# Filler matmuls ahead of the transposes in a recurrence on TensorE

## What is computed

```python
def rec_step(carry, inp):
    R, h = carry
    zt, kt, vt, bt = inp
    qh = softmax(h)
    v_old = einsum('bhij,bhj->bhi', R, kt)
    R = R + (bt * (vt - v_old))[..., :, None] * kt[..., None, :]
    h = zt + einsum('bhij,bhj->bhi', R, qh)
    return (R, h), h
```

## Time and profile before

| what | us |
|---|---|
| runs, device time | 18266.01, 18280.08, 18282.9 |
| median | 18280.08 |
| profiled execution, span first to last instruction | 18228.0 |
| median less that span | 52.1 |
| recurrence, 9936 to 14770 in the span | 4834 |
| one run, prologue included | about 604 |

### The profile page before, as it was taken

The page is one execution under the profiler, slowest core; times in us unless marked ns, Lnnn a source line. Parts: engine busy times, 40 slices in busy tenths (PEclk is TensorE's granted clock), DMA queues, the critical chain, the costliest instruction groups (busy, mean ns, idle before and its releaser), DMA issues. The chain is left out here.

```text
span 18228.0 us, 593330 instructions
## 1 busy us (share of the span) xinstructions
PE 13070.7 (72%) x262069; PEld 10252.8 (56%) x262069; DVE 10572.6 (58%) x24424; ACT 6554.5 (36%) x16019; POOL 2261.8 (12%) x1394
## 2 busy tenths in 40 slices
PE   4607778770866999999997766776677676867777
PEld 3504566660544777777775555555555565645555
DVE  6451457774125666666666777666767645446664
ACT  3101236550213666666664221111112122345541
POOL 0038200003461111111111000000000000000001
PEclk9556568875867999999998766776687697967775
DMA  0313320121332111111112112201220152177652
GB/s 20 110 26 49 72 48 21 34 76 33 72 59 67 28 25 27 28 26 27 27 26 51 21 38 45 44 19 38 45 44 19 38 149 79 45 237 195 193 135 65
DMA packets 1835030, 1095.27 MB, mean 60 GB/s; under 512 B 1109166, under 2 KB 1763409, under 8 KB 1814481
## 3 DMA queue, kind: packets, MB, share of 16 engines
q1 hardware_dynamic: 1605063, 999.32, 22.7%
q0 software_dynamic: 227328, 57.19, 2.1%
HBM read 569.43 MB, written 484.53 MB: 58 GB/s over the span
## 5 line engine op out<-in xcount | busy, mean ns | idle before, releaser
L2894 PE MATMUL recur_acc<-recur_U,recur_W 8*32 8x64 f32 (+4 forms) x49152 | 1406.2, 270 | 504.8 <-ACT recur_W L2816 429.9
L2894 PEld LDWEIGHTS recur_acc<-recur_U,recur_W 8*32 8x32 f32 (+4 forms) x49152 | 1071.1, 140 | 924.5 <-ACT recur_W L2816 741.8
L2945 DVE TENSOR_TENSOR recur_pr<-recur_K,recur_e 124x64 f32<-124x64 f32 (+60 forms) x1024 | 1282.0, 1252 | 395.8 <-ACT recur_e L2828 395.6
L2881 PE MATMUL recur_acc<-recur_R,recur_E 128*32 128x64 f32 x62976 | 1212.6, 233 | 243.2 <-issue 232.7
L2950 DVE TENSOR_REDUCE recur_dot<-recur_pr 124x1 f32<-124x64 f32 (+60 forms) x1024 | 1281.6, 1252 | 29.7
L2881 PEld LDWEIGHTS recur_acc<-recur_R,recur_E 128*32 128x32 f32 x62976 | 1078.3, 118 | 343.5 <-issue 288.1
L2816 ACT ACTIVATE recur_W<-recur_wT 128x256 f32<-128x256 f32 (+16 forms) x1024 | 336.1, 328 | 1969.9 <-PE recur_wT L2866 1968.8
L2866 PE MATMUL recur_wT<-const_ident,recur_w 128*128 128x128 f32 (+15 forms) x1536 | 480.8, 375 | 768.5 <-DVE recur_w L2954 762.1
L2475 ACT ACTIVATE delta_B1l<-delta_pS 64x256 f32<-64x256 f32 x1968 | 745.1, 379 | 704.5 <-PE delta_pS L2375 679.9
L2475 ACT ACTIVATE delta_B0l<-delta_pS 64x256 f32<-64x256 f32 x1968 | 745.6, 379 | 620.9 <-PE delta_pS L2375 600.5
L2510 POOL TENSOR_TENSOR delta_QK<-delta_QK,delta_mx 128x512 f32<-128x512 f32 x369 | 380.3, 1045 | 3038.1 <-DVE delta_mx L2563 3038.0
(11 more groups left out here) (620 smaller groups left out, 33946.8 us busy)
## 6 DMA issues: line engine op xcount, KB each, us to landing
scr<-rel_BD SPq DMA_DIRECT2D x128, 1288.0 KB
rel_sc<-scr SPq DMA_DIRECT2D x128, 861.0 KB
xnT<-ln_xT SPq DMA_DIRECT2D x64, 492.0 KB, 3.0
kr<-delta_QK SPq DMA_DIRECT2D x492, 64.0 KB, 2.3
ur<-delta_Uf SPq DMA_DIRECT2D x492, 64.0 KB, 2.2
zz<-delta_Z SPq DMA_DIRECT2D x492, 64.0 KB, 2.2
recur_K<-kr SPq DMA_DIRECT2D x64, 448.0 KB
recur_H<-zz SPq DMA_DIRECT2D x64, 448.0 KB
```

The lines of the kernel that those rows point to most:

```text
L2881: nc.tensor.matmul(acc[a][32 * q:32 * q + 32, 0:FD], E[a][:, EQ * q + 32 * j:EQ * q + 32 * j + 32], R[a][:, m, :], start=(j == 0), stop=False)
L2894: ins = nc.tensor.matmul(acc[a][32 * q:32 * q + 32, 0:FD], W[a][0:8 * k, b, 160 * q + 32 * j:160 * q + 32 * j + 32], U[a][0:8 * k, 2 * (t ...
L2945: V.tensor_tensor(pr[0:cp, 0:n, :], K[a][0:cp, r0:r0 + n, :], e[a][0:cp, None, :].to_broadcast([cp, n, FD]), ALU.mult).then_inc(s_own[a], 1)
```

## The change

A bfloat16 tile `keep` of zeros, 128 partitions by 384 columns, is added and set to zero once, before the first run; SyncE's wait ahead of the first load counts one memset more. A new function `stay_busy(a, t)` issues k matmuls on TensorE, with 32 columns of `keep` as weights and all 384 as the moving operand, into the first 32 partitions of columns 128 to 511 of `recur_eT`, which nothing reads.

In the first pass it stands ahead of `turn(a, t)`, from n = 12 on, and waits until the product of the dots of (a, t) is done (`s_own[a]` at 4t + 2); k is 5 at n = 12, 7 at n = 16, 9 at n = 20, 10 at n = 24, 12 at n = 28 and 13 at n = 32. In the second pass it stands between `state(a, t)` and `turn(a, t)`, without a wait; k is 1 at n = 22, 2 at n = 24, 5 at n = 28 and 8 at n = 32. Per group and run this is 197 and 50 matmuls.

```diff
+        keep = st.sb("keep", [128, 384], BF16)
+        filler = lambda a: eT[a][0:32, 128:512]
...
-                sp.wait_ge(s_own[0], 14)
+                sp.wait_ge(s_own[0], 15)
...
-                zeros = [t for a in range(2) for t in (W[a], E[a], U[a], w[a], ed[a], wT[a])]
+                zeros = [t for a in range(2) for t in (W[a], E[a], U[a], w[a], ed[a], wT[a])] + [keep]
...
+                    def stay_busy(a, t):
+
+                        n = t % HC + 1
+                        if t < HC:
+                            k = int((0.067 * n + 0.15) / 0.165) if n >= 12 else 0
+                            if k:
+                                pe.wait_ge(s_own[a], 4 * t + 2)
+                        else:
+                            k = int(max(0.0, 0.06 * n - max(0.0, 2.6 - 0.067 * n)) / 0.165)
+                        for _ in range(k):
+                            nc.tensor.matmul(filler(a), keep[:, 0:32], keep[:], start=True, stop=True)
+
                     for t in range(SL):
...
                         if t < HC:
                             for a in range(2):
+                                stay_busy(a, t)
                                 turn(a, t)
...
                             state(0, t)
+                            stay_busy(0, t)
                             turn(0, t)
                             recent(0, t, lambda: turn_exp(1, t))
                             state(1, t)
+                            stay_busy(1, t)
                             turn(1, t)
```

## The result

Fifteen runs of the changed kernel have a median of 18321.34 us (18292.66 to 18419.62), fifteen of the kernel before 18283.31 us (18266.01 to 18298.38). The ratio is 1.0025, with a 95% interval of 1.0016 to 1.0034: 38 us slower. The forecast was 24 us faster.

What follows compares the result with a forecast made beforehand. It took first-pass steps as bound by TensorE at 1.2 GHz in a loop through ScalarE and VectorE, with VectorE binding at pass ends. Terms -13.2 + 1.5 + 6.5 - 1.1 + 3.3 = -3.0 a run; 18280 - 24 = 18256 us, range 18205 to 18310.

Steps and rivals of the forecast that it cites:

- the wide one: Range for the whole kernel's time, 18190 to 18370 us, leaving out the no-clock rival and the tail of the gain.
- the second pass that pays: Rival: second-pass fillers' time is on the path, in full 128 us over eight runs, 18360 us; chance 0.13.
- the full-clock gain of the first pass: First-pass steps from t = 14, 18 steps, get shorter at 2.4 GHz: -13.2 us a run.
- (a): First pass, t = 11 to 13: fillers still run at 0.32 us each, +1.5 us a run.
- (b): First pass: a tenth of 14 steps fall to the low clock, swing 4.6 us: +6.5 us a run, bounds 0 and 13.
- (c): First state product of the second pass: 3.06 us on the low clock, 1.99 on the high one, -1.1 us a run.
- second-pass fillers: Second pass: 100 fillers take 16 us a run, a fifth of it on the path: +3.3 us a run.
- The rival in which the clock does not rise: Rival: 32-column fillers of zeros do not raise the first pass's clock and cost 0.32 us each: 18790 us; chance 0.12.
- the first part of such a step: First pass, t = 19, group 0's turn to group 1's turn: 4.31 us with nine fillers, against 5.08: -0.77.
- 5.3 against 5.5 to 5.9: Second pass from t = 60: TensorE's half step 5.3 us plus remaining issue waits, VectorE's 5.5 to 5.9; nearly even.
- The 52 us: Whole kernel: profiled span 18228.0 us lies 52 us under the median of the runs; taken as unchanged.

Runs made afterwards that it cites:

- e13: e1 with two more fillers in each half step from t = 12, between turn and recent: 18147.18 us, ratio 0.9957.
- e1: The changed kernel with the first pass's fillers alone, none in the second pass: 18218.7 us, ratio 0.9993.
- e2: The changed kernel with the second pass's fillers alone, none in the first pass: 18261.0 us, ratio 1.0016.
- e8: The changed kernel again, unaltered, beside other kernels and on another chip: 18251.3 us, ratio 1.0014.
- e12: The changed kernel once more, unaltered, beside other kernels and on another chip: 18266.72 us, ratio 1.0015.
- e3: The changed kernel with only group 0's fillers in the first pass and none in the second: 18142.99 us, ratio 0.995.
- e4: The kernel before, without fillers, make_state moved behind group 1's recent and its ScalarE reader one step later: 18093.48 us, ratio 0.9925.
- e15: e14 with group 0's filler count in t = 15 to 30 smaller by 1 instead of by 6: 18044.56 us, ratio 0.9904.
- e14: e10 with two more fillers in each half step from t = 12, between turn and recent: 18158.33 us, ratio 0.996.
- e9: The changed kernel with the first pass's fillers 8 columns long, same number of instructions: 18293.48 us, ratio 1.0039.
- e10: e4 with both groups' first-pass fillers, group 0's count smaller by 6 in t = 15 to 30: 18261.41 us, ratio 1.0017.

## Why the prediction was wrong

The sign was wrong, +38 us for -24. The 18321 lie above the forecast's own range of 18205 to 18310 (which takes its two bounds one at a time; both together would have given 18346) and inside the wide one. Of the rivals, the second pass that pays is the one a part of which came true. Two terms failed, and each miss is about as large as the whole forecast gain of 3.0 us a run: the full-clock gain of the first pass was too large, and the second pass, of whose fillers I put four fifths at nothing, costs more. By its own terms, in us a run:

| term | predicted | measured | from |
|---|---|---|---|
| t = 14 to 31 at the full clock | -13.2 | -10.4 | 182.3 against 192.7; e13 182.7 |
| (a) cold fillers, t = 11 to 13 | +1.5 | +2.3 | 21.9 against 19.6 |
| (b) dips | +6.5 | +5.9 | 188.2 less 182.3; e1 5.6 |
| (c) state product at t = 32 | -1.1 | 0.0 | below |
| second-pass fillers | +3.3 | +3 to +4; in the whole kernel +5 to +7 | e2; e8, e12 and the first measurement, less the first pass; (c) is in it |
| sum | -3.0 | +3.3 to +4.8 | medians: 26, 34 and 38 us over eight runs |
| of it, first pass without (c) | -5.2 | -1.2 to -2.2 | 266.7, 266.4 and 265.7 against 267.9 |
| of it, second pass with (c) | +2.2 | +5 to +7 | as two rows above |

**The clock** was called rightly: 0.50 to 0.90, a filler at 0.163 us (nine in 1.64 with the last's modelled end) and 0.32 cold. The rival in which the clock does not rise is out.

**The full-clock gain** was too large by 2.8. (The middle of the values that I listed for the steps would even be some -14.) At t = 19 it is 10.74 to 9.68, -1.06 where I had -1.3; from t = 21 to 24 the steps gain 0.9 to 0.4, where I had 1.1 to 0.8. My sum for the first part of such a step was 4.31 us; in the timeline after, from 10707.40 to the turn at 10712.11, it is 4.71:

```profile
10708.31 1.24 PE L2896 MATMUL recur_acc<-recur_U,recur_W 128*32 128x64 f32 x64 [0.47 <-ACT recur_W L2818]
...
10709.47 1.15 PE L2910 MATMUL recur_Rp<-recur_Us,recur_Ks 32*64 32x64 f32 x32
...
10710.55 1.64 PE L2923 MATMUL recur_eT<-recur_keep 128*32 128x384 bf16 x9
...
10712.11 0.44 PE L2868 MATMUL recur_wT<-const_ident,recur_w 128*128 128x128 f32 x2
```

Start to start, `recent` takes 1.16 where I halved it to 1.01, `make_state` 1.08 where I had 0.95, and the nine fillers 1.56 where I had 1.44. None of them quite halves. The mechanism stands: group 1's fillers are on the path behind `make_state`, as e3 shows by leaving them out. What I did with it was too little. I wrote that "the change pays half its gain back" and did not ask what `make_state` itself does in that place; e4 says 18 us a run. And e3, with group 1's fillers left out and most steps dipped, has a first pass of 255.0 us, shorter than the 259.5 of e13 at the full clock.

**The dips** came out near the sum by luck. I had a tenth of the steps at a swing of 4.6 us; it is nearly a third (44 of 144), each partly cold, at 1.1 us apiece. I took them as a given of the engine's clock, from the 0.92 and 0.96 of the second pass. They depend on what is issued: e13 ended them with two more fillers a half step, e15 with five more a step than e14.

**(c)** fell to "issue" waits, which the prediction set against the fillers alone and not against this product. PE at the start of the second pass, t = 32, in the changed kernel:

```profile
10826.00 1.31 PE L2883 MATMUL recur_acc<-recur_R,recur_E 128*32 128x64 f32 x77 [0.47 <-ACT recur_E L2824]
10828.52 0.89 PE L2883 MATMUL recur_acc<-recur_R,recur_E 128*32 128x64 f32 x47 [1.21 <-issue]
10829.34 0.27 PE L2868 MATMUL recur_wT<-const_ident,recur_w 128*8 128x128 f32 x1
```

The passes are now at 2.4 GHz, and 1.21 us of "issue" stands in their middle: 3.34 us from start to turn, where the product of the earlier trace rows took 3.06. I read that row as cold; in the trace the clock rises inside it, at 10809.76, and a product with 0.50 throughout takes 3.57 to the turn (e3, second run). Over the eight runs it is 1.92 to 5.12 us from start to turn in the changed kernel, 3.6 in the mean, against 2.9 before, and the step t = 32 takes 8.49 against 8.53. What the clock gave, the wait took. It need not: in e15, also at the full clock, all eight take 1.92 and the step 6.45. PE at t = 32 of its second run:

```profile
10766.20 1.99 PE L2883 MATMUL recur_acc<-recur_R,recur_E 128*32 128x64 f32 x124 [0.47 <-ACT recur_E L2824]
```

Why the wait stands there in one kernel and not in the other is open.

**The second pass**, its fillers and (c) together, I had at +2.2 us a run; it is +5 to +7 in the whole kernel. A fifth of the fillers' 16 us was near what they cost alone (2.8 us in the profile of e2, 4.0 by its medians), but for other reasons. Late in the pass the issue waits did give way, though by little: from t = 53 to 63 they are 16.8 us a run before, 13.1 in e2 and 13.0 to 15.2 in the whole kernel. VectorE's slack from t = 60 on was smaller than "5.3 against 5.5 to 5.9": with eight fillers TensorE comes 2.0 to 3.1 us after `w` in the last half step. In the last step nothing follows into which lateness could go, and the fillers of both groups there add 2.4 us (e2); t = 53 to 62 add another 2.1 (t = 32 to 52, which have one or no filler, are 1.8 shorter in that profile, which is its scatter). The rival "second pass pays in full" stays off: 16 us a run were needed for it, 3 to 7 are there.

**The 52 us** between span and median were no property of the kernel: in the five later measurements it took 18223 to 18233 us, near the 18228.0 of its profile. What made it slower in the first measurement is not known. Taken as unchanged in the difference of two medians, the 52 did no harm; but the 339.3 beside the 328.3 of the second pass in the first table is no like-for-like pair, and the +5 to +7 above do not use it.

What stays open is why the second pass costs more in the whole kernel (333.4 to 339.3) than with its own fillers alone (331.1). e9 excludes the position of the instructions alone. Longer "issue" waits hold a part of it (0.8 to 5.4 us a run more than in e2), and what lengthens them is not known. The scatter of single profiles may hold some: the profile of e8 is 13 us slower than its median and that of e12 14, e2's 6 us slower; but that of the first measurement is 6 us faster.

## What to carry to other kernels

When fillers are to hold TensorE's clock, a short wait can be the place for them: here two more fillers in a wait of 0.47 us were the difference between 0.9993 and 0.9957. But put them only where the engine waits for another in every step, and none where it is itself late: leaving out group 1's, with a lower clock, gave as much (0.995, e3). So first look whether real work, like `make_state`, stands on the path and could fill the wait instead, since that gave 0.75% at a granted clock of 0.50. Leave fillers out of the last step of a loop, where in e2 they cost 2.4 us a run, and be wary of them where the profile shows "issue" waits.

## What the runs showed of the hardware

- Fillers on 8 rows held TensorE busy 238 of 260 us and left the granted clock at 0.50; on 128 rows, all zeros and 32 columns wide, the same count brought 0.92. I had not expected the rows in use to matter.
- With fillers before each turn and behind it the full clock held from t = 14 to 31 (1.00 over 182 and 169 us in e13 and e15), though idle stretches of up to 1.22 us were left at a step of e13. In e10 1.56 us idle before a turn preceded the fall. In e10 a step at a mean granted clock of 0.69 took 2.7 us more than one on the full clock (11.34 against 8.61 at t = 19).
- A bfloat16 matmul of 384 columns takes 0.163 us, start to start in a burst, at 2.4 GHz and 0.320 at 1.2 GHz; one of 8 columns takes 0.027 us at 1.2 GHz (e9), and nine of them delayed the turn by 0.33.
- A state product at t = 32 took, from its start to the turn, 3.57 us at 1.2 GHz (e3, second run) and 1.92 at 2.4 GHz (all eight in e15). In the changed kernel, at 2.4 GHz, it took 3.34 in the second run, of which 1.21 are "issue".
